# Narrow experts scatter their weighted rows into two sums by token, in place of a stage of 128 gathers

## The chip, the cores and the metric

The kernel runs on one core of a Trainium2 chip. A core has a matrix engine (TensorE, in the profile PE, with its weight loads as PEld), a vector engine (VectorE, DVE), an activation engine (ScalarE, ACT), GpSimd (POOL) and SyncE (SP), which issues most of the transfers. GpSimd issues the indirect transfers, those whose rows are picked by a list of row numbers. Sixteen DMA engines carry all transfers. The engines run side by side and wait for each other by semaphores. The metric is the device time of one execution in microseconds (us), the median of the runs.

## The reference

Four layers of cross attention and feed-forward over x, 2048 tokens of 256 numbers. The change touches the feed-forward of layer 0 (64 experts, 8 for each token, hidden width 192, at most 128 tokens an expert, beside one shared expert) and the cross attention of layer 1, which reads its result:

```
probs = softmax(x @ router_w.T);  topk_w, topk_ids = top_k(probs, 8);  topk_w /= sum(topk_w)
pos   = place of this choice among the choices of the same expert;  valid = pos < 128
idx   = topk_ids * 128 + pos                      # the slot; a token without one is dropped
x_buf[idx] = x[tok]
h = silu(x_buf @ w_gate) * (x_buf @ w_up);  y = h @ w_down           # for each expert's 128 slots
routed = segment_sum(y[idx] * topk_w * valid, tok)
x = x + routed + shared_expert(norm(x))
x = x + L1_attention(norm(x), ctx_1024)
```

## The kernel before

x stays in on-chip memory as 16 tiles of 128 tokens (`all_x`, in code `k.x`). The program is a row of stages, each a block in which every engine runs its own list and at whose end all engines meet; `begin_stage` and the SP loop of `sem_clear` free the semaphores of the last one.

**a0** (`low_rank_attention`) is the attention of layer 0, the routing of its experts and the shared expert. One loop over `step` runs all of them with a lag for each: VectorE ranks tile t in step t+6 (`rank_top` to `rank_sum`), TensorE counts it in step t+7 (`count`, which reads `chosen` and the running total `sofar`), VectorE makes its slots in step t+8 (`pick` to `place`), and GpSimd then scatters the tile's normalized rows eight times, once for each choice (`scatter`), into the slot buffer `m_xbuf` in DRAM. GpSimd also takes the power of each tile's variance (`power`, result `a_rstd`), four steps before. `rank_chosen(t)` waits for `count(t-1)`, since `chosen` and `sofar` have two buffers. Behind the loop come the shared expert (`shared_gate_up`, `hide`, `shared_down`, `add_shared`) and the weights of all tiles at once.

**m0e** (`narrow_experts`) goes over 32 pairs of experts. SP waits for all scatters, then loads a pair's rows (`load_x`, 256 KB), its gate and up weights (`load_gu`, 768 KB) and its down weights (`load_d`, 384 KB). TensorE turns the rows, makes gate and up and, two steps later, down. VectorE copies the result to `y`, and GpSimd stores it to `m_ybuf` (256 KB, one transfer a pair).

**m0c** (`combine`) gathers for every token its eight result rows: GpSimd issues 16 x 8 indirect reads of 128 rows, VectorE multiplies each by its weight and adds it to x. Beside them, in the same block, `fold_contexts` prepares the layers 1 to 3: TensorE and ACT fold the context into 33 heads' weights, SP stores them, and behind the last head SP loads three rows that VectorE splits into bf16 parts. In VectorE's list this split stands behind all adds.

**n** (`norm_scales`) takes mean and power for all tiles. **a1** (`attention`, no experts of its own) is a `pipeline` over the tiles: norm (lag 0), scores (1), masks, maxima and exp (2), output (3). A hardware loop runs its middle steps. SP has nothing to do in it but load the fold at its start and then the first weights of the next stage (`local.load_first`). The attention behind M2 (**a3**) has `combine_before` in its loop already: it gathers two rows a token and adds them in the same pipeline, all its own phases two steps later (`lag = 2`).

What orders the work is the written order of each list and the semaphores; there is no planner.

Of the kernel before, what the change touches and what calls it, by code (L numbers as in the profile page):

```python
# [360 lines left out]
def zero_slot_buffers(k, pool, names):  # L361

    for name in names:
        if name in k.slot_buffers:
            xbuf, zeroed, n, tile = k.slot_buffers[name]
            for i in range(n):
                pool.dma_start(xbuf[i * 4 * tile:(i + 1) * 4 * tile, :].rearrange("(p a) d -> p (a d)", p=tile), k.zeros[0:tile, :]).then_inc(zeroed, 16)


class Ahead:  # L370
# [3 lines left out]
    def __init__(self, k, m, d):  # L374
# [6 lines left out]
        if m is M0:  # L381
            self.slots, self.weights = s.sb("slots", [P, T, m.top], U32), s.sb("weights", [P, T, m.top])
            s = Scope(k, self.early, m.name + "w")
            self.xn_t = s.sb("xnall", [P, DC, T * P])
            self.top, self.pos = s.sb("top", [P, T, 8]), s.sb("pos", [P, T, m.top])
            self.rows = [s.sb(f"rows{i}", [P, D]) for i in range(6)]
            self.scattered = s.lasting_sems("scattered", len(self.rows))
            self.wgu = [s.sb(f"wgu{i}", [P, 2 * DC, 2 * m.hidden]) for i in range(4)]
            self.wgu_in = s.lasting_sems("wguin", len(self.wgu))
        self.wr, self.logits = s.sb("wr", [P, DC, m.e]), s.sb("logits", [P, T, m.e])  # L390
# [10 lines left out]
    def wait_scattered(self, eng):  # L401
        n = len(self.rows)
        for i in range(n):
            eng.wait_ge(self.scattered[i], 16 * self.m.top * len(range(i, T, n)))

# [43 lines left out]
def attention(nc, k, a, d):  # L449
# [6 lines left out]
    with ExitStack() as ctx:  # L456
# [61 lines left out]

        if before:
            K = before.m.top  # L520
# [5 lines left out]
            combined = s.steps("combined", *(f"{i}" for i in range(K)), "stats", "copy", "aggr", "mean", "eps")  # L526
# [7 lines left out]
        with nc.Block() as block:  # L534
            @block.sync
            def _(sp):
# [27 lines left out]
            def _(dve):  # L564
# [15 lines left out]
                def combine_before(t, u):  # L580
# [3 lines left out]
                    for i in range(K):  # L584
                        nc.vector.scalar_tensor_tensor(row(k.x, t), got[u][:, i, :], before.weights[:, bass.ts(t, 1), i], row(k.x, t),
                                                       ALU.mult, ALU.add).then_inc(combined.sem, 1)
                        done(f"{i}")
# [92 lines left out]
                masks = [(2, mask_scores if a.mask == "tokens" else mask_keys)] if a.mask else []  # L680
                if ahead:
                    for st in (renormed, logged):
                        dve.sem_inc(st.sem, 2 * st.n)
                    if before:
                        for st in (indexed, combined):
                            dve.sem_inc(st.sem, 2 * st.n)
                        for u in range(2):
# [2355 lines left out]
```

## Time and profile before

| | us |
|---|---|
| median of 3 runs | 2836.45 (2835.34 to 2838.21) |
| the profiled execution | 2839.5 |
| its span | 2837.7 |
| TensorE busy in it | 2382.7 (84%) |
| VectorE, ACT, GpSimd busy | 1223.7, 1067.9, 608.6 |
| granted TensorE clock, mean | 0.881 of 2.4 GHz |

The span runs from the first instruction to the last. The stages of the change lie in its first quarter: a0 from 0 to 303 us, m0e to 499, m0c to 690, n to 693, a1 to 762. A busy share tells how long an engine worked, not whether anything waited for it; that stands in the rows below, in the idle time before an instruction and what ended it.

### The profile page before, as it was taken

Reading aid. Unit: us, or ns where it says so; the run is one execution under the profiler, and the core shown is the slowest. Engines: PE = TensorE matmul, PEld = TensorE weight load, DVE = VectorE, ACT = ScalarE, POOL = GpSimd, SP = SyncE. Lnnn points to the kernel's source line nnn. Section 1 sums busy time; section 2 is a strip of 40 time slices with the busy share of each in tenths; the row PEclk is TensorE's granted clock in tenths of the full one; section 3 lists DMA queues with packets and bytes.
Section 4 is the critical chain, followed back from the end, with each engine's and each line's share of the span. In section 5 each row is a group of like instructions: output and inputs, shape, how many; then the busy total and the mean of one; then the engine's idle time right before and its main releaser. Section 6 shows DMA issues by size and latency. Waiting matters only on the chain. (4 is left out here: it accounts for less than half of the span.)

```text
span 2837.7 us, 44374 instructions
## 1 busy us (share of the span) xinstructions
PE 2382.7 (84%) x13334; PEld 1720.2 (61%) x13367; DVE 1223.7 (43%) x3165; ACT 1067.9 (38%) x3643; POOL 608.6 (21%) x638
## 2 busy tenths in 40 slices
PE   6996899880879989899989799549997998099991
PEld 3774577550456755467655466449985566099991
DVE  3674222344657753266743344512222564332223
ACT  2551222340256652166642255223332554033440
POOL 3277211674032110012110000130001220400004
PEclk7987999765599999999999899769998999599996
DMA  9200697542040020000000500311013300511113
GB/s 324 80 13 29 197 305 223 170 125 64 33 141 10 10 55 0 31 8 10 11 6 0 186 21 0 118 61 31 29 30 126 131 14 10 169 36 35 37 35 95
DMA packets 162724, 213.46 MB, mean 75 GB/s; under 512 B 36732, under 2 KB 140171, under 8 KB 161400
## 3 DMA queue, kind: packets, MB, share of 16 engines
q1 hardware_dynamic: 133320, 150.16, 16.8%
q0 software_dynamic: 29264, 61.54, 6.5%
q8 instruction: 74, 1.21, 0.2%
q14 instruction: 66, 0.54, 0.1%
HBM read 150.96 MB, written 83.52 MB: 83 GB/s over the span
## 5 line engine op out<-in xcount | busy, mean ns | idle before, releaser
L2321 POOL TENSOR_TENSOR la_invnorm<-la_clamped,all_minushalf 128x16 f32<-128x16 f32 x32 | 92.9, 2902 | 541.8 <-DVE la_clamped L2393 541.8
L819 PE MATMUL a_score_bank<-a_fold,a_xnt 128*128 (+3 forms) x448 | 183.7, 537 | 0.0
L846 PE MATMUL a_out_bank<-a_vw,a_probst 128*128 (+5 forms) x672 | 169.9, 406 | 3.6 <-ACT a_probst L755 3.4
L738 ACT ACTIVATE a_probs<-a_score_bank,a_mx 128x77 f32<-128x77 f32 x528 | 162.1, 363 | 3.4 <-DVE a_mx L633 2.6
L2048 ACT ACT_TABLE_LOAD x40 | 51.3, 1283 | 287.8 <-PE m3e_h_bank L2021 152.6
L2021 PE MATMUL m2e_h_bank<-m2e_xt,m2e_w1e 128*128 128x108 f32 x1280 | 152.0, 278 | 0.1
L2021 PE MATMUL m3e_h_bank<-m3e_xt,m3e_w1e 128*128 128x128 f32 x1280 | 151.7, 277 | 0.0
L2021 PEld LDWEIGHTS m2e_h_bank<-m2e_xt,m2e_w1e 128*128 128x128 f32 x1280 | 148.6, 195 | 0.5 <-DVE m2e_xt L2062 0.5
L2021 PEld LDWEIGHTS m3e_h_bank<-m3e_xt,m3e_w1e 128*128 128x128 f32 x1280 | 148.5, 194 | 0.1
L846 PEld LDWEIGHTS a_out_bank<-a_vw,a_probst 128*128 128x128 f32 (+2 forms) x672 | 129.7, 200 | 28.2 <-issue 6.8
L2031 PE MATMUL m2e_y_bank<-m_w,m2e_ht 128*108 x640 | 144.6, 379 | 0.0
L2031 PE MATMUL m3e_y_bank<-m_w,m3e_ht 128*128 x640 | 144.6, 379 | 0.0
L2471 ACT ACTIVATE la_probs<-la_score_bank,la_nb,la_invnorm 128x256 f32<-128x256 f32 x256 | 140.8, 576 | 5.8 <-DVE la_nb L2411 5.7
L2101 POOL DMA_INDIRECT m0c_got<-m_ybuf,m0c_slot x128 | 129.7, 1013 | 51.6 <-issue 44.5
L1008 POOL DMA_INDIRECT m_xbuf<-m0w_rows,m0w_slots x128 | 127.4, 995 | 37.6 <-issue 37.3
L738 ACT ACTIVATION_READ_ACCUMULATOR a_probs<-a_score_bank,a_mx 128x1 f32 x528 | 129.2, 245 | 0.0
L2031 PEld LDWEIGHTS m3e_y_bank<-m_w,m3e_ht 128*128 128x128 f32 x640 | 118.6, 190 | 14.5
L2031 PEld LDWEIGHTS m2e_y_bank<-m_w,m2e_ht 128*108 128x108 f32 x640 | 107.8, 173 | 24.1
L2048 ACT ACTIVATE m3e_ht<-m3e_h_bank,m3w_b 128x128 f32<-128x128 f32 x320 | 89.3, 376 | 85.9 <-PE m3e_h_bank L2021 85.7
L2048 ACT ACTIVATE m2e_ht<-m2e_h_bank,m2w_b 128x108 f32<-128x108 f32 x320 | 84.1, 359 | 89.5 <-PE m2e_h_bank L2021 89.2
L819 PEld LDWEIGHTS a_score_bank<-a_fold,a_xnt 128*128 128x128 f32 x448 | 82.0, 213 | 52.4 <-issue 42.1
L709 POOL DMA_INDIRECT a_got<-m_ybuf,a_slot x32 | 32.8, 1025 | 359.9 <-DVE a_slot L578 311.3
(444 smaller groups left out, 4839.1 us busy)
## 6 DMA issues: line engine op xcount, KB each, us to landing
m0w_wgu<-in_m_gu SPq DMA_DIRECT2D x32, 768.0 KB, 5.6
m_xbuf<-all_zeros POOLq DMA_DIRECT2D x36, 512.0 KB, 19.2
m_w<-in_m_w SPq DMA_DIRECT2D x16, 1024.0 KB, 12.3
m_xbuf<-all_zeros POOLq DMA_DIRECT2D x20, 432.0 KB, 11.8
m0e_wd<-in_m_down SPq DMA_DIRECT2D x32, 256.0 KB, 5.1
m0e_xb<-m_xbuf SPq DMA_DIRECT2D x32, 256.0 KB, 5.7
m_ybuf<-m0e_y POOLq DMA_DIRECT2D x32, 256.0 KB, 4.8
m2w_w<-in_m_w SPq DMA_DIRECT2D x8, 1024.0 KB
```

The lines of the kernel that those rows point to most:

```text
L709: nc.gpsimd.indirect_dma_start(got[u][:, i, :], None, before.ybuf[:, :], bass.IndirectOffsetOnAxis(slot[u][:, i:i + 1], 0), bounds_check=b ...
L738: last = nc.scalar.activation(probs[u][:, h * J:(h + 1) * J], score_ps[g][:, (h - h0) * J:(h - h0 + 1) * J], ACT.Exp, bias=mx[u][:, h:h + ...
L819: last = nc.tensor.matmul(score_ps[g][:, (hs[0] - h0) * J:(hs[-1] + 1 - h0) * J].rearrange("p (h j) -> p h j", j=J), xn_t[u][:, c, :], fol ...
L846: last = nc.tensor.matmul(out_ps[:, 0:D], probs_t[u][0:n, c, :], vw[0:n, bass.ds(b, 1), c, :].rearrange("p o n -> p (o n)"), start=False, ...
L1008: nc.gpsimd.indirect_dma_start(k.slot_buffers[m.name][0][:, :], bass.IndirectOffsetOnAxis(ahead.slots[:, t, i:i + 1], 0), ahead.rows[t % R ...
L2021: last = nc.tensor.matmul(h_ps[u][half][:, i * R:(i + 1) * R], w1[u][:, c, f0:f0 + P], xt[u][:, c, :], start=c == 0, stop=c == DC - 1)
L2031: last = nc.tensor.matmul(y_ps[u][0:R, 0:D], h_t[u][:, c, :], r.w2[:, bass.ts(e, 1), c, :].rearrange("p o f -> p (o f)"), start=c == 0, st ...
L2048: last = nc.scalar.activation(h_t[u][:, 4 * half + i, :], h_ps[u][half][:, i * R:(i + 1) * R], m.act, bias=r.ahead.b1[:, bass.ds(e * HC + ...
L2101: nc.gpsimd.indirect_dma_start(got[u][:, j, i, :], None, r.ybuf[:, :], bass.IndirectOffsetOnAxis(slot[u][:, j, i:i + 1], 0), bounds_check= ...
L2321: nc.gpsimd.tensor_tensor(inv_norm[t % 2][:, :], clamped[t % 2][:, :], k.minus_half[:, :], ALU.pow).then_inc(powered.sem, 1)
L2471: last = nc.scalar.activation(probs[u][:, hh, :], score_ps[j][:, i * 2 * P:(i + 1) * 2 * P], ACT.Exp, bias=nb[u][:, hh:hh + 1], scale=inv_ ...
```

## The change

The expert stage no longer stores its results by slot. Each row of `m_xbuf` grows from 256 to 288 numbers (`PAYLOAD`): behind the token's row it carries the eight expert numbers, the eight weights and the token's number. In m0e VectorE finds in a loaded row the weight that belongs to this expert and the token (`find`, `found_at`; an empty slot gets one of 128 spare rows), multiplies the result by the weight (`copy_y`), and GpSimd scatters it with an adding transfer into one of two DRAM tensors of 2560 rows by token, `sums[0]` for the first expert of a pair and `sums[1]` for the second. Two adds into one tensor must not overlap, so each waits for the one before. The sums start as x (stored by SP at the end of a0) and zero. m0c is left with the folds alone (`fold_stage`), n goes, and a1 loads both sums tile by tile and adds them (`combine_before` with `summing`).

In a0 the weights are made tile by tile (`rank_shift`, `soften`, `carry`), `sofar` has three buffers and `rank_chosen(t)` waits for `count(t-2)`, and the first two of four parts of the shared expert's gate and up move into the last steps of the loop.

```diff
@@ a0, SP, behind the first weights
                 for q in range(len(ahead.wgu)):
                     ahead.load_gate_up(sp, q)
+                ahead.wait_scattered(sp)
+                for q in range(len(ahead.xb)):
+                    ahead.load_rows(sp, q)
+                sp.wait_ge(ahead.sum_zeroed, 96)
+                for p in range(T // 2):
+                    sp.wait_ge(shared_added, p + 1)
+                    sp.dma_start(ahead.sums[0][1 + 2 * p * P:1 + 2 * (p + 1) * P, :].rearrange("(t p) d -> p t d", p=P),
+                                 k.x[:, 2 * p:2 * p + 2, :]).then_inc(ahead.x_stored, 16)
@@ a0, GpSimd, behind the zeroing of the slots
+                for i, total in enumerate(ahead.sums):
+                    for c in range(0 if i else SUM_ROWS // 512 - 1, SUM_ROWS // 512):
+                        pool.dma_start(total[c * 512:(c + 1) * 512, :].rearrange("(p a) d -> p (a d)", p=P), k.zeros[:, 0:4 * D]).then_inc(ahead.sum_zeroed, 16)
...
                 def scatter(t):
                     pool.wait_ge(placed, t + 1)
+                    pool.wait_ge(weighing, 2 * (t + 1))
@@ a0, VectorE
+                def carry(t):
+                    dve.wait_ge(softened, t + 1)
+                    nc.vector.reciprocal(sum_top[t % 2][:, :], sum_top[t % 2][:, :]).then_inc(weighing, 1)
+                    nc.vector.tensor_scalar(ahead.rows[t % R][:, IDS], idxf[t % 3][:, :], 1.0, None, ALU.add)
+                    nc.vector.tensor_copy(ahead.rows[t % R][:, TOKEN], k.token[:, t:t + 1])
+                    dve.wait_ge(weighing, 2 * t + 1)
+                    nc.vector.tensor_scalar(ahead.rows[t % R][:, WEIGHTS], exped_top[t % 2][:, :], sum_top[t % 2][:, 0:1], None, ALU.mult).then_inc(weighing, 1)
...
                 def rank_chosen(t):
                     dve.wait_ge(ranked, 5 * t + 4)
-                    if t >= 1:
-                        dve.wait_ge(counted, t)
-                        dve.wait_ge(summed, t)
+                    if t >= 2:
+                        dve.wait_ge(counted, t - 1)
@@ a0, TensorE, in the loop over the steps
+                    if step == T + 3:
+                        pe.wait_ge(shared_in, 48)
+                        pe.wait_ge(exped, NG * T)
+                        pe.wait_ge(p_copied, 3 * T)
+                        shared_gate_up(0)
+                    if step == T + 6:
+                        pe.wait_ge(added, T)
+                        pe.wait_ge(logged, T)
+                        shared_gate_up(1)
@@ m0e, SP
                 def load_x(q):
-                    if q >= NX:
-                        sp.wait_ge(turned, q - NX + 1)
-                    sp.dma_start(xb[q % NX][:, :, :], r.xbuf[q * 2 * P:(q + 1) * 2 * P, :].rearrange("(i p) d -> p i d", p=P)).then_inc(x_in[q % NX], 16)
+                    sp.wait_ge(turned, q - NX + 1)
+                    sp.wait_ge(found, 2 * (q - NX + 1))
+                    r.ahead.load_rows(sp, q)
@@ m0e, GpSimd
                 for q in range(npair):
                     pool.wait_ge(y_copied, q + 1)
-                    pool.dma_start(r.ybuf[q * 2 * P:(q + 1) * 2 * P, :].rearrange("(i p) d -> p i d", p=P), y[q % 2][:, :, :]).then_inc(stored[q % 2], 16)
-                for u in range(2):
-                    pool.wait_ge(stored[u], 16 * (npair // 2))
+                    for i in range(2):
+                        if q >= 1:
+                            pool.wait_ge(summed[i], 16 * q)
+                        nc.gpsimd.indirect_dma_start(sums[i][:, :], bass.IndirectOffsetOnAxis(dest[q % NY][:, i:i + 1], 0), y[q % NY][:, i, :], None,
+                                                     bounds_check=SUM_ROWS - 1, oob_is_err=True, compute_op=ALU.add).then_inc(summed[i], 16)
@@ m0e, VectorE
                 def copy_y(q):
                     dve.wait_ge(y_made, q + 1)
-                    if q >= 2:
-                        dve.wait_ge(stored[q % 2], 16 * (q // 2))
-                    nc.vector.tensor_copy(y[q % 2][:, :, :].rearrange("p i d -> p (i d)"), y_ps[q % 2][:, :]).then_inc(y_copied, 1)
+                    dve.wait_ge(found, 2 * (q + 1))
+                    for i in range(2):
+                        last = nc.vector.tensor_scalar(y[q % NY][:, i, :], y_ps[q % 2][:, i * D:(i + 1) * D], weight[q % NY][:, i:i + 1], None, ALU.mult)
+                    last.then_inc(y_copied, 1)
@@ a1, SP
+                if summing:
+                    for i in range(2):
+                        sp.wait_ge(before.ahead.summed[i], 16 * (M0.ntiles // 2))
+                    def load_sums(t, u):
+                        sp.wait_ge(combined.sem, combined.at(t - 2, "x"))
+                        for i in range(2):
+                            sp.dma_start(got[u][:, i, :], before.ahead.sums[i][bass.ds(t * P + 1, P), :]).then_inc(gathered[u], 16)
+                    pipeline(sp, T, (0, load_sums))
                 if local:
                     local.load_first(sp)
@@ a1, VectorE
-                    pipeline(dve, T, *later((0, norm), *masks, (2, maxima), (2, scale), (3, add)))
+                    pipeline(dve, T, *later((0, norm), *masks, (2, maxima)), *combine_first, *later((2, scale), (3, add)))
```

Three places show how instructions move. First SP's list at the end of a0 and the start of m0e, before (L408 is `load_gate_up`, L1836 `load_x`):

```order
L408 DMA m0w_wgu<-in_m_gu 128x4x384 x4
L961 UNCONDITIONAL_BRANCH
L1828 UNCONDITIONAL_BRANCH
...
L1847 DMA m0e_wdrest<-in_m_down 64x2x256
L1836 DMA m0e_xb<-m_xbuf 128x2x256 x5
```

and in the change (L1038 stores x into the first sum):

```order
L419 DMA m0w_wgu<-in_m_gu 128x4x384 x4
L415 DMA m0w_xb<-m_xbuf 128x2x288 x4
L1038 DMA m_sum<-all_x 128x2x256 x8
L1004 UNCONDITIONAL_BRANCH
L1912 UNCONDITIONAL_BRANCH
...
L1931 DMA m0e_wdrest<-in_m_down 64x2x256
L415 DMA m0w_xb<-m_xbuf 128x2x288
L419 DMA m0w_wgu<-in_m_gu 128x4x384
```

The first four loads of rows move ahead of the seam between the stages (the two branches) and of the down weights, and eight stores stand between them and the seam.

GpSimd's list from m0e to the end of m0c, before:

```order
L1862 DMA m_ybuf<-m0e_y 128x2x256 x32
L1827 UNCONDITIONAL_BRANCH
L2092 UNCONDITIONAL_BRANCH
...
L2101 DMA m0c_got<-m_ybuf,m0c_slot 128x256
L2098 REGISTER_ALU
```

and in the change:

```order
L1948 DMA m_sum<-m0e_y,m0e_dest 2560x256 x64
L1911 UNCONDITIONAL_BRANCH
L724 UNCONDITIONAL_BRANCH
L730 TENSOR_TENSOR all_rstd<-all_var,all_minushalf 128x1
L83 UNCONDITIONAL_BRANCH
```

32 stores become 64 adds, the 128 gathers are gone, and L730 takes the power of a tile's variance in a1.

VectorE's list for one step of a1 (the last one ahead of the hardware loop, from the masks on), before:

```order
L622 TENSOR_TENSOR a_score_bank<-a_score_bank,a_factor 128x77
L624 TENSOR_TENSOR a_score_bank<-a_score_bank,a_addend 128x77
L633 TENSOR_REDUCE a_mx<-a_score_bank 128x1
L639 RECIPROCAL a_inv<-a_total 128x1
L641 TENSOR_TENSOR a_probs<-a_probs,a_inv 128x77
L645 TENSOR_TENSOR all_x<-all_x,a_out_bank 128x256
L647 BN_STATS all_stats<-all_x 128x6
```

and in the change:

```order
L659 TENSOR_REDUCE a_mx<-a_score_bank 128x1
L606 TENSOR_TENSOR all_x<-a_got 128x256
L614 BN_STATS all_stats<-all_x 128x6
L617 COPY a_stb<-all_stats 128x6
L620 BN_AGGR a_mvb<-a_stb 128x2
L623 COPY all_mean<-a_mvb 128x1
L624 TENSOR_SCALAR all_var<-a_mvb 128x1
L665 RECIPROCAL a_inv<-a_total 128x1
L667 TENSOR_TENSOR a_probs<-a_probs,a_inv 128x77
L671 TENSOR_TENSOR all_x<-all_x,a_out_bank 128x256
```

Six instructions, each waiting for the one before, move in between the maximum and the reciprocal of every step.

## Rows read from the trace of the kernel before

**Rows 1.** Stretches of a0's loop, of m0c's fold and of a1.

```profile
core 0: us, PE busy (x) PEld busy (x) DVE busy (x) ACT busy (x) POOL busy (x), PEclk, DMA share, GB/s
124.00:203.00 79.00, 78.89 (x428) 56.17 (x426) 60.62 (x191) 42.04 (x165) 62.01 (x64) 0.87 0.09 27
507.00:632.00 125.00, 122.90 (x548) 78.03 (x548) 49.27 (x110) 55.37 (x185) 95.95 (x95) 0.69 0.50 151
699.00:762.00 63.00, 55.38 (x176) 33.47 (x176) 36.46 (x128) 17.20 (x65) 0.00 (x0) 0.50 0.28 91
```

**Rows 2.** GpSimd in order of time, a0: start, duration, then idle time and its releaser.

```profile
124.41 1.10 POOL L1008 DMA_INDIRECT m_xbuf<-m0w_rows,m0w_slots  x1 [0.19 <-issue]
...
191.54 0.89 POOL L1003 TENSOR_TENSOR a_rstd<-a_ve,all_minushalf 128x1 f32<-128x1 f32 x1 [0.17 <-DVE a_ve L1109]
...
296.80 0.97 POOL L1008 DMA_INDIRECT m_xbuf<-m0w_rows,m0w_slots  x1 [0.30 <-issue]
```

**Rows 3.** VectorE in order of time, one step of a0's loop.

```profile
189.60 1.04 DVE L1144 TENSOR_REDUCE a_chosen<-a_onehot 128x64 bf16<-128x512 f32 x1 [2.82 <-issue]
...
191.31 0.14 DVE L1109 TENSOR_SCALAR a_ve<-a_mv 128x1 f32<-128x1 f32 x1
```

**Rows 4.** SP's issues in order of time, first of m0e.

```profile
303.47 0.37 SPq L1846 DMA_DIRECT2D m0e_wd<-in_m_down  x1
...
308.69 6.66 SPq L1836 DMA_DIRECT2D m0e_xb<-m_xbuf  x5
```

**Rows 5.** TensorE in order of time, first of m0e.

```profile
313.85 1.97 PE L1876 MATMUL m0e_turned_bank<-all_ident,m0e_xb 128*128 128x128 f32 x8 [13.56 <-DMA m0e_xb<-m_xbuf]
```

**Rows 6.** One y store of m0e, in GpSimd's order of time.

```profile
459.80 0.72 POOL L1862 DMA_DIRECT2D m_ybuf<-m0e_y  x1 [4.87 <-DVE m0e_y L1948]
```

**Rows 7.** A stretch inside m0e, columns as in rows 1.

```profile
330.00:386.00 56.00, 56.00 (x362) 42.57 (x360) 14.34 (x30) 13.51 (x30) 7.18 (x10) 1.00 1.02 308
```

**Rows 8.** DMA between 325 and 500 us, rate in 40 equal slices.

```profile
GB/s 347 345 311 289 305 329 315 306 287 309 315 325 285 288 326 302 317 291 300 320 320 307 278 320 319 287 304 288 336 315 288 303 306 314 28 37 60 60 60 60
```

**Rows 9.** From issue to landing: the 32 stores of m0e's y.

```profile
DMA to landing us min/median/max: 2.5/4.8/6.0
```

**Rows 10.** From issue to landing: the 128 scatters of a0.

```profile
DMA to landing us min/median/max: 2.1/2.2/3.6
```

**Rows 11.** GpSimd in order of time, the last gather of m0c.

```profile
676.41 1.00 POOL L2101 DMA_INDIRECT m0c_got<-m_ybuf,m0c_slot  x1 [0.30 <-issue]
```

**Rows 12.** TensorE in order of time, first of the fold.

```profile
506.93 1.39 PE L290 MATMUL m0c_kv_bank<-all_ctxt,m0c_a1wk 128*128 128x154 f32 x4 [12.54 <-DMA m0c_a1wo<-in_a_wo]
```

**Rows 13.** ACT in order of time, last of the fold.

```profile
632.24 0.57 ACT L340 COPY m0c_vwout<-m0c_v_bank 77x512 f32<-77x512 f32 x1
```

**Rows 14.** VectorE in order of time, end of m0c, stage n, a1's first norm.

```profile
683.41 0.15 DVE L349 CAST m0c_a1part<-m0c_a1row 82x5 bf16<-82x5 f32 x1
...
686.08 0.18 DVE L357 CAST m0c_a3part<-m0c_a3rest 85x32 bf16<-85x32 f32 x1
690.85 1.17 DVE L158 BATCH_NORM_AGGREGATE all_mv<-all_stats 128x2 f32<-128x6 f32 x16 [4.59 <-PEq L2091]
...
698.92 0.73 DVE L605 TENSOR_SCALAR a_xn<-all_x,all_mean,all_rstd 128x256 f32<-128x256 f32 x2
```

**Rows 15.** VectorE in order of time, one step of a1's loop.

```profile
719.53 0.42 DVE L645 TENSOR_TENSOR all_x<-all_x,a_out_bank 128x256 f32 x1 [0.32 <-PE a_out_bank L846]
...
721.47 0.24 DVE L633 TENSOR_REDUCE a_mx<-a_score_bank 128x1 f32<-128x77 f32 x1
722.19 0.16 DVE L639 RECIPROCAL a_inv<-a_total 128x1 f32<-128x1 f32 x1 [0.48 <-ACT a_probs L738]
...
723.16 0.42 DVE L645 TENSOR_TENSOR all_x<-all_x,a_out_bank 128x256 f32 x1 [0.54 <-PE a_out_bank L846]
```

**Rows 16.** VectorE in order of time, the same chain in a3's loop.

```profile
2314.01 0.48 DVE L585 SCALAR_TENSOR_TENSOR all_x<-a_got,all_m2weights,all_x 128x256 f32 x1 [0.16 <-DVE all_x L585]
...
2316.08 0.15 DVE L598 TENSOR_SCALAR all_var<-a_mvb 128x1 f32 x1
2316.30 0.17 DVE L654 COPY a_st<-all_stats 128x6 f32 x1
```

More of the change, by code:

```diff
@@ L517, in attention @@
             routed, logged = s.steps("routed"), s.steps("logged")
+        summing = before is not None and before.m is M0
         if before:
-            K = before.m.top
+            K = 2
             got, slot = s.pair("got", [P, K, D]), s.pair("slot", [P, K], U32)
@@ L525, in attention @@
             indexed, scaled_before = s.steps("indexed"), s.steps("scaledbefore")
-            combined = s.steps("combined", *(f"{i}" for i in range(K)), "stats", "copy", "aggr", "mean", "eps")
+            combined = s.steps("combined", *(("x",) if summing else ("0", "x")), "stats", "copy", "aggr", "mean", "eps")
         def later(*phases):
@@ L583, in combine_before @@
                     dve.wait_ge(gathered[u], (t - u) * (8 * K) + 16 * K)
[L584 to L587, printed above, removed]
+                    if summing:
+                        nc.vector.tensor_tensor(row(k.x, t), got[u][:, 0, :], got[u][:, 1, :], ALU.add).then_inc(combined.sem, 1)
+                    else:
+                        for i in range(K):
+                            if i:
+                                done("0")
+                            nc.vector.scalar_tensor_tensor(row(k.x, t), got[u][:, i, :], before.weights[:, bass.ts(t, 1), i], row(k.x, t),
+                                                           ALU.mult, ALU.add).then_inc(combined.sem, 1)
+                    done("x")
                     nc.vector.bn_stats(row(k.stats, t), row(k.x, t)).then_inc(combined.sem, 1)
@@ L680, in _ @@
                 masks = [(2, mask_scores if a.mask == "tokens" else mask_keys)] if a.mask else []
+                index_first, combine_first = ([(0, index)], [(1, combine_before)]) if before else ([], [])
+                if before:
+                    for st in (indexed, combined):
+                        dve.sem_inc(st.sem, 2 * st.n)
+                    if summing:
+                        index_first = []
+                    else:
+                        for u in range(2):
+                            nc.vector.memset(got[u][:, :, :], 0.0).then_inc(cleared, 1)
                 if ahead:
@@ L1021, in _ @@
                 nc.vector.memset(none3[:, :], 0.0)
+                for rows in ahead.rows:
+                    nc.vector.memset(rows[:, D:PAYLOAD], 0.0)
                 nc.vector.tensor_copy(before16[:, :], k.before[:, :])
@@ L1955, in narrow_experts, with fold_stage @@
         r.old_sems.close()
+def fold_stage(nc, k, jobs):
+    with ExitStack() as ctx:
+        with nc.Block() as block:
+            fold_contexts(nc, k, Scope(k, ctx, "m0c"), block, jobs)
 def wide_experts(nc, k, m, d, r):
@@ L2156, in experts @@
         r.xbuf, r.zeroed, r.nzero, _ = k.slot_buffers[m.name]
-        r.ybuf = nc.dram_tensor(f"{m.name}_ybuf", (m.rows, D), F32, kind="Internal").ap()
+        if m is not M0:
+            r.ybuf = nc.dram_tensor(f"{m.name}_ybuf", (m.rows, D), F32, kind="Internal").ap()
         r.iota, r.before, r.ones = k.iota, k.before, k.ones
         r.m = m
-        if m is M0:
-            r.slots, r.weights = k.ahead.slots, k.ahead.weights
-        elif m is M2:
+        if m is M2:
             r.slots, r.weights = k.m2_slots, k.m2_weights
-        else:
+        elif m is M3:
             r.slots, r.weights = s.sb("slots", [P, T, m.top], U32), s.sb("weights", [P, T, m.top])
```

233 lines of the change are left out of this document (143 added, 90 removed).

## The prediction

> **What bounds the kernel now.** I read the stretches by window first, since each stage of the change has a limit of its own. In a0's loop TensorE is busy for 78.89 of 79 us, GpSimd for 62.01 [rows 1]: it is TensorE's loop. In m0e TensorE is again never idle (56.00 of 56), but the DMA engines are busy all the time too, share 1.02 at 308 GB/s [rows 7], so two limits lie side by side. In the fold TensorE works 122.9 of 125 us at a clock of 0.69, in a1 55.38 of 63 at 0.50, which is the lower level, 1.2 GHz [rows 1].
>
> Then the rows at the seams, for who comes last. From the last scatter to TensorE's first turn in m0e 17 us pass, of which TensorE waits 13.56 for the rows [rows 2, 5]. The fold's last copy ends at 632.8 [rows 13], but the split behind it stands in VectorE's list behind all adds, whose last gather is issued at 676.41 [rows 11]; it runs at 683.41 [rows 14]. So m0c ends with the chain of gathers and adds, 50 us after the fold. That tail is where time can be had.
>
> **Part 1, a0's loop.** GpSimd's scatters wait for slots, these for `chosen`, and that for the last count: 2.82 us of wait in one step [rows 3]. The power at 191.54 is the last thing in GpSimd's list that waits for VectorE; from there the scatters run back to back to 296.80 [rows 2]. So only what makes the list late before 191.54 counts. The wait of 2.82 goes; `carry` puts four small instructions ahead of the slots and takes back some 0.3. Term: -2.5 us (ends -3 and 0). Rows of 288 numbers in place of 256 are 12.5% more bytes; an issue of 0.97 to 1.10 us [rows 2] is work on 128 row numbers, not on bytes, so I cost it at 0; were it by bytes, 128 x 0.12 = +15 us, which I keep for the range. The early zeroing (about 4 MB more in a0) has nobody waiting and 0.09 of the DMA engines in use [rows 1]: 0. The two parts of the shared expert that move into the loop take its end ahead of the last scatter; a loop that TensorE bounds grows by them, but GpSimd, not TensorE, ends the stage: 0.
>
> **Part 2, the seam.** From 296.80 to 313.85 it is 17.05 us [rows 2, 5]. Now SP waits for the scatters (landing 2.2 [rows 10]) and issues four loads and eight stores before it meets the others; eight issues took 5.22 us (303.47 to 308.69 [rows 4]), so 12 x 0.65 = 7.8, and some 0.7 for the seam itself. The rows have landed by then. 2.2 + 7.8 + 0.7 = 10.7: term -6.3 (ends -9 and -3). What is late next is SP itself with its stores.
>
> **Part 3, m0e.** A pair takes 0.72 + 4.87 = 5.59 us [rows 6] and moves 768 + 256 + 128 KB of weights, 256 of rows in and 256 of y out, 1664 KB, 305 GB/s, which fits the 308 of the row. Now the rows are 288 KB, and an add reads its destination too: 1696 + 256 = 1952 KB. The trace has no adding transfer, so bounds. The best rate in m0e is 347 GB/s [rows 8]; 1952 KB at 346 is 5.78 us, +0.19 for each of 32 pairs, +6. If TensorE's 5.59 hides everything, 0. If an add costs its bytes once more (2208 KB), 6.53 us, +30. Slices of 345 are the first two only, when buffers are empty; the others lie at 285 to 335, so I take 5.95, that is 336 GB/s: +12 (ends 0 and +30).
>
> A rule of the Trainium skill bears on this ("Collectives: The Full Stack", The bandwidth ceiling): a reducing transfer is slower than a copy not for the addition but because it reads two sources, one descriptor for each. By that rule it is 1952 KB and +6; no row here shows an add, and my +12 does not rest on it.
>
> Beside the rate there is a chain. Each add waits for the last one into its tensor, so each of the two tensors must take its 128 KB within a period. A y store of 256 KB lands in 4.8 us under this load and at most in 6.0 [rows 9], a scatter of 128 rows under light load in 2.2 [rows 10]. With a landing under 5.5 the chain is hidden; I take it as hidden, at about 5 us, near the store's 4.8. GpSimd's issues, 2 x 1.0 us, fit. VectorE's extra (`find`, `found_at`) too: it worked 14.34 of 56 us [rows 7].
>
> The Trainium skill ("DMA: Bandwidth & Descriptors", Anatomy of one DMA) gives 2.0 us and the bytes at 436 GB/s for one: 2.3 us for 128 KB and 2.6 for twice that. The scatter's 2.2 agrees, the store's 4.8 does not, since it has no load of others in it; the chain would by it be hidden with room to spare.
>
> **Part 4, the seam to the fold.** The fold's first matmul stands 12.54 us idle, on a weight load [rows 12], behind a stage end at which GpSimd waited for y stores. That wait goes to a1: -1.5 (ends -4, 0).
>
> **Part 5, m0c.** TensorE's fold is as long as before and its clock, with TensorE busy 98%, the same. From its last copy at 632.8: store and reload of rows, two issues and landings of 2.2 to 2.5 each, 5.5 in all; the splits 683.41 to 686.26, 2.85; to the next block 4.59 [rows 14]. 632.8 + 5.5 + 2.85 + 4.6 = 645.75, where it was 690.85: -45 (ends -40, -52). What is late next is the fold itself. The last adds have landed 130 us earlier.
>
> **Part 6, n and a1.** Stage n goes, 8.07 us from 690.85 to a1's first norm at 698.92 [rows 14]. In its place a1 waits for the loads of the sums (an issue, a landing of 2.2), sum, statistics and power before its first norm, about 8 as well: 0. In its loop a step takes 3.63 us, add to add [rows 15]: 2.18 from the add to the end of the maximum, 0.48 of wait for ACT's exp, 0.97 to the next add, of which 0.54 is waiting for TensorE. The sum, the copies and statistics come behind the maximum, each waiting for the one before; in a3 the same chain takes 2.3 us (2314.01 to 2316.30) [rows 16]. It covers both waits: 2.18 + 2.3 + 0.49 = 4.97 with the 0.54 gone and 0.48 covered, about 1.3 a step more. Term: 15 x 1.3 = +19.5 (ends: it hides further in waits, +8; it hides in nothing, 15 x 2.3 = +34). The first weights of the next stage are issued behind 14 tiles' loads, some 20 us later in a stage that then lasts over 80: hidden (0, +3).
>
> **Sum.** -2.5 - 6.3 + 12 - 1.5 - 45 + 19.5 = -23.8 us against the profiled execution's 2839.5. The median of the runs is 2836.45, 0.1% under it, so I take the difference from that: 2812.6.
>
> **Rival 1, the adds cost nothing.** TensorE never waits in m0e, and a share of 1.02 with rates up to 347 [rows 7, 8] does not prove a full limit. Then m0e stays at 5.59 a pair and the term of +12 goes: 2836.45 - 35.8 = 2801. Against it: the rate falls whenever buffers are full, and 17% more bytes come.
>
> **Rival 2, slower: the chain of adds is the bound.** Each add reads, adds and writes 128 rows of 1 KB in the full queues of m0e; if its landing is over the period, period = landing + 0.3, and the pairs stretch, TensorE waits for `y` buffers or rows. Without Part 3 the rest gives -35.8, so it turns to slower from a period of 5.59 + 35.8/32 = 6.71, a landing of 6.4. For it: the store reached 6.0 with one trip to memory [rows 9], an add needs two. At a landing of 7.3, +64.6 - 35.8 = +29: 2865. Against it: it is half the bytes of the store.
>
> **Rival 3, the steps of a1 hide nothing** and the first weights come late: +34 + 3 in place of 19.5, 2830; with scatters 12% dearer it would be 2845. For it: a chain of six dependent instructions on an engine that is already the slow one with TensorE at 0.50. Against it: the waits are in the rows.
>
> **Chances.** Forecast (2805 to 2825) 0.46, rival 1 (2795 to 2805) 0.18, rival 3 (2826 to 2840) 0.12, rival 2 (2837 and up) 0.17, anything else 0.07, spread on both sides. 0.2%, 5.7 us, is what can be told from no change here. Faster by more: forecast, rival 1 and nearly all of the 2830s short of 2830.8 (0.08), with some of the rest, 0.77; within 0.2% 0.05; slower 0.18. The range 2792 to 2846 leaves out some 0.13 above and 0.04 below; the forecast's own is 2805 to 2825.
>
> **What would show it.** First scatter and power of tile 6 about 2.5 us earlier; TensorE's first turn of m0e near 305, with SP issuing stores right up to it; period of pairs 5.8 to 6.1, with TensorE's idle time put down to weights or rows (rate limit), not to `y` (chain): GpSimd waiting for its own add before nearly every issue, at a period equal to the landing, would prove rival 2. The fold's end then 45 us nearer to a1; a1's step at 4.9 with no idle before the reciprocal; the first weights of the stage behind a1 landed before it begins. It is wrong if m0e's period stays 5.6 or passes 6.5, or a1's step passes 5.5.

## The result, and the profile after

| | before | changed |
|---|---|---|
| median, 8 runs each | 2836.69 us | 2849.79 us |
| range | 2833.29 to 2843.23 | 2842.42 to 2859.85 |
| time to before | | 1.0045 (95%: 1.0028 to 1.0062) |
| span of the profiled execution | 2837.7 | 2848.2 |

Slower by 0.45%, where 2812.6 was forecast: the range that was given held neither the time nor, with its 0.77 for faster, the direction. The mechanism that decides is the second rival, the chain of adds. These are the points in time in both profiled executions, from rows like those below ([rows 2, 5, 12 to 14] for before); the differences add up to the spans' 10.5 us.

| | before | changed | difference | forecast |
|---|---|---|---|---|
| start to first scatter | 124.4 | 118.9 | -5.5 | none |
| first to last scatter | 172.4 | 170.4 | -2.0 | -2.5 |
| to the first matmul of m0e | 17.05 | 11.17 | -5.9 | -6.3 |
| m0e's matmuls | 180.5 | 218.5 | +38.0 | +12 |
| their end to the fold | 12.5 | 27.6 | +15.1 | -1.5 |
| fold to a1's first norm | 192.0 | 148.0 | -44.0 | -45 |
| a1, first norm to last addition | 62.5 | 76.9 | +14.4 | +19.5 |
| the rest | 2076.3 | 2076.7 | +0.4 | 0 |

The changed kernel's GpSimd list in the middle of m0e, in order of time (start, duration, then the idle time before it and what ended it):

```profile
376.99 1.54 POOL L1948 DMA_INDIRECT m_sum<-m0e_y,m0e_dest  x1 [5.68 <-DMA m_sum<-m0e_y,m0e_dest]
378.83 1.54 POOL L1948 DMA_INDIRECT m_sum<-m0e_y,m0e_dest  x1 [0.30 <-issue]
384.75 1.54 POOL L1948 DMA_INDIRECT m_sum<-m0e_y,m0e_dest  x1 [4.38 <-DMA m_sum<-m0e_y,m0e_dest]
386.60 1.54 POOL L1948 DMA_INDIRECT m_sum<-m0e_y,m0e_dest  x1 [0.30 <-issue]
392.36 1.54 POOL L1948 DMA_INDIRECT m_sum<-m0e_y,m0e_dest  x1 [4.22 <-DMA m_sum<-m0e_y,m0e_dest]
```

In [rows 6] the idle time ahead of the store was ended by VectorE's result. Here it is ended by GpSimd's own last add. A pair takes 392.36 - 384.75 = 7.61 us where it took 5.59; from 376.99 to 506.98 us seventeen pairs take 7.65 each. The two adds of the list go into different tensors. These are the views of the one at 384.75, into the tensor of the pair's second expert, and of the one at 386.60, into the first's:

```profile
L1948 POOL DMA_INDIRECT m_sum<-m0e_y,m0e_dest x1: 1541/1541/1541, 384.8 to 384.8; - x1
...
DMA to landing us min/median/max: 6.8/6.8/6.8
```

```profile
L1948 POOL DMA_INDIRECT m_sum<-m0e_y,m0e_dest x1: 1541/1541/1541, 386.6 to 386.6; - x1
...
DMA to landing us min/median/max: 5.8/5.8/5.8
```

The first of them lands at 391.6 (landings are counted from the start of the issue), and the next add into its tensor is issued 0.8 us later, at 392.36: 6.8 + 0.8 is the period. The other tensor has 1.8 us to spare. So one of the two chains sets the pace. The view of that line over all of m0e says how long an add takes and who waited for it:

```profile
L1948 POOL DMA_INDIRECT m_sum<-m0e_y,m0e_dest x64: 1532/1540/1575, 313.0 to 534.2; - x64
...
  DMA m_sum<-m0e_y,m0e_dest: 110.9, 32
...
  DVE m0e_weight L2047: 120.6, 23
  POOL m_sum L1948: 110.9, 32
DMA to landing us min/median/max: 3.6/6.2/8.8
```

The landing, 6.2 us in the median (6.5 between 320 and 500 us), stands where [rows 9] have 4.8 for a store of twice the bytes. GpSimd waited 110.9 us for it, and VectorE 120.6: `found_at` waits for the adds of four pairs ago before it writes `weight` and `dest`. That wait stands ahead of `hide` in VectorE's list, so `hide`, with which TensorE goes on, comes late although its data are there:

```profile
391.71 0.17 DVE L2047 TENSOR_REDUCE m0e_weight<-m0e_picked 128x2 f32<-128x16 f32 x1 [5.70 <-DMA m_sum<-m0e_y,m0e_dest]
391.80 0.15 DVE L2048 TENSOR_TENSOR m0e_dest<-m0e_spot,m0w_xb 128x2 uint32<-128x2 f32 x1
391.86 0.41 DVE L2026 TENSOR_TENSOR m0e_hrest<-m0e_gaterest,m0e_gu_bank 64x256 f32<-64x256 f32 x1
```

By windows, the columns as in [rows 1], the stretch of [rows 7] and the next one, changed kernel:

```profile
330.00:386.00 56.00, 54.56 (x335) 41.84 (x334) 17.49 (x79) 12.13 (x27) 22.80 (x15) 0.94 0.90 252
386.00:440.00 54.00, 47.35 (x263) 35.42 (x262) 13.33 (x64) 10.20 (x23) 22.41 (x16) 0.91 0.85 232
```

The DMA share falls from 1.02 to 0.85 and the rate from 308 to 232 GB/s. So it is not the engines' rate that ran out; they wait too. Behind the last matmul GpSimd still has a backlog: matmul, last add, and TensorE's first matmul of the fold:

```profile
518.22 0.70 PE L1986 MATMUL m0e_y_bank<-m0e_wdrest,m0e_hrest 64*128 64x256 f32 x2
```

```profile
534.19 1.54 POOL L1948 DMA_INDIRECT m_sum<-m0e_y,m0e_dest  x1 [0.30 <-issue]
```

```profile
546.57 1.39 PE L290 MATMUL m0c_kv_bank<-all_ctxt,m0c_a1wk 128*128 128x154 f32 x4 [27.65 <-DMA m0c_a1wo<-in_a_wo]
```

The last add is issued 15.3 us behind the last matmul (518.92), and no engine leaves the stage before it: the fold's first load is issued at 540.76. That is the +15.1.

The other side, ACT's last copy of the fold and VectorE's split:

```profile
670.75 0.58 ACT L340 COPY m0c_vwout<-m0c_v_bank 77x512 f32<-77x512 f32 x1
```

```profile
676.48 0.17 DVE L349 CAST m0c_a1part<-m0c_a1row 82x5 bf16<-82x5 f32 x1 [155.38 <-DMA m0c_a3row<-a_dram_row]
...
694.55 0.41 DVE L631 TENSOR_SCALAR a_xn<-all_x,all_mean,all_rstd 128x256 f32<-128x256 f32 x1 [0.75 <-POOL all_rstd L730]
```

The split follows the fold by 5.1 us, where 50.6 lay between [rows 13, 14]; 5.5 was forecast. The stage did lose its tail.

a1, VectorE in order of time, from one addition to the next:

```profile
712.78 0.41 DVE L671 TENSOR_TENSOR all_x<-all_x,a_out_bank 128x256 f32 x1
...
714.69 0.24 DVE L659 TENSOR_REDUCE a_mx<-a_score_bank 128x1 f32<-128x77 f32 x1
714.91 0.43 DVE L606 TENSOR_TENSOR all_x<-a_got 128x256 f32 x1
...
716.89 0.15 DVE L624 TENSOR_SCALAR all_var<-a_mvb 128x1 f32 x1
716.96 0.15 DVE L665 RECIPROCAL a_inv<-a_total 128x1 f32<-128x1 f32 x1
717.15 0.24 DVE L667 TENSOR_TENSOR a_probs<-a_probs,a_inv 128x77 f32<-128x77 f32 x1
717.30 0.41 DVE L671 TENSOR_TENSOR all_x<-all_x,a_out_bank 128x256 f32 x1
```

The waits for ACT and TensorE in [rows 15] are gone; the chain of the sum takes 2.1 us (714.91 to 717.04). From 712.78 to 755.54 nine steps take 4.75 us each, where 3.63 to 3.78 stood.

### The profile page after: what moved, and what is told of

The parts are those of the page before. It is cut to its first block and busy times, and to the rows that moved or that the text cites. A ratio compares the mean times of both kernels' runs of the same rounds, so it can differ in the third digit from the quotient of the medians.

```text
span 2848.2 us, 44375 instructions
## 1 busy us (share of the span) xinstructions
PE 2407.0 (85%) x13366; PEld 1735.3 (61%) x13367; DVE 1192.0 (42%) x3352; ACT 1065.6 (37%) x3670; POOL 565.2 (20%) x564
## 3 DMA queue, kind: packets, MB, share of 16 engines
q1 hardware_dynamic: 140392, 157.51, 16.9%
## 5 line engine op out<-in xcount | busy, mean ns | idle before, releaser
L777 ACT ACTIVATE a_probs<-a_score_bank,a_mx 128x77 f32<-128x77 f32 x528 | 161.7, 360 | 16.9 <-DVE a_mx L659 16.8
L1948 POOL DMA_INDIRECT m_sum<-m0e_y,m0e_dest x64 | 98.6, 1541 | 146.9 <-DMA m_sum<-m0e_y,m0e_dest 110.9
L2528 DVE TENSOR_REDUCE la_mx<-la_score_bank 128x2 f32<-128x512 f32 x128 | 87.7, 685 | 48.2 <-PE la_score_bank L2670 48.2
```

What stands on the lines that cost most here:

```text
L777: last = nc.scalar.activation(probs[u][:, h * J:(h + 1) * J], score_ps[g][:, (h - h0) * J:(h - h0 + 1) * J], ACT.Exp, bias=mx[u][:, h:h + ...
L1948: nc.gpsimd.indirect_dma_start(sums[i][:, :], bass.IndirectOffsetOnAxis(dest[q % NY][:, i:i + 1], 0), y[q % NY][:, i, :], None, bounds_che ...
L2528: nc.vector.tensor_reduce(mx[u][:, h0:h1 + 1:2], score_ps[j][:, :].rearrange("p (h e) -> p h e", h=2), AX, ALU.max).then_inc(maxed.sem, 1)
```

## The experiments

All against the kernel before in the same set. What follows of the stages is read from one trace for each. m0e's matmuls hardly vary from one to the next (180.5 to 181.9 us wherever the stall is gone); the first scatter does (117.7 to 129.0 us).

**e1, e2: more tensors for the sums.**

The waits of `found_at` and the loads and additions of a1 follow the number of tensors.

```diff
-                        if q >= 1:
-                            pool.wait_ge(summed[i], 16 * q)
-                        ...(sums[i][:, :], ..., compute_op=ALU.add).then_inc(summed[i], 16)
+                        e = 2 * q + i
+                        o = e % NSUM                      # 3 in e1, 4 in e2
+                        if e >= NSUM:
+                            pool.wait_ge(summed[o], 16 * (e // NSUM))
+                        ...(sums[o][:, :], ..., compute_op=ALU.add).then_inc(summed[o], 16)
```

> Expert e adds into tensor e mod 3 of three, in place of two; an add waits for the one three experts earlier; the attention behind loads and adds three sums. Theory A (the chain: a tensor's next add waits for the last one's landing, 6.95 us from issue and 0.6 to the next issue, 7.55 us a pair) : the limit falls to 7.55 x 2/3 = 5.0 us a pair, so the pairs go by the matmuls or the DMA engines, 5.6 to 6.1 us; from the first to the last matmul of m0e 218 us becomes 182 to 197, and the backlog of adds behind the last matmul (17 us) is nearly gone; a1 gains one more addition a step, +0.5 x 16 = 8 us. Total 2849 - 30 - 13 + 8 = about 2810 to 2820. Theory B (the DMA engines cannot move the bytes of the adds faster): m0e stays at 218 us and the total rises by 8.

> Four tensors, an add waits for the one four experts earlier. Theory A: the chain allows 3.8 us a pair, nothing is left of it; m0e is as with three tensors or 1 to 3 us shorter, a1 8 us longer than with three, total 2815 to 2828. Theory B: m0e 218 us as with two.

e1: 2812.21 us, time to before 0.991 (0.9891 to 0.9929). e2: 2821.05 us, 0.9933 (0.9913 to 0.9953). m0e's matmuls take 180.5 and 181.7 us, what they took before the change. The waits of line L1958 (the add) in e1 and its landing:

```profile
  DVE m0e_y L2064: 62.0, 25
  DMA m_sum<-m0e_y,m0e_dest: 24.6, 17
  issue: 12.3, 22
...
DMA to landing us min/median/max: 3.7/6.8/8.6
```

and the window of m0e again, e1, beside which the kernel before had 1.00 and 307 in the last two columns:

```profile
386.00:440.00 54.00, 54.00 (x347) 41.02 (x347) 19.88 (x90) 13.23 (x30) 29.31 (x20) 1.00 1.10 316
```

The landing is as long as before, 6.8 us, and TensorE never waits, since GpSimd now waits for VectorE's result, and 24.6 us for adds instead of 110.9. Theory B, that the engines can't move the bytes of the adds faster, falls: 316 GB/s at a share of 1.10 go through, with the same adds. a1 got 7.0 us longer with the third sum (83.9) and another 7.3 with the fourth (91.2), so three is the better number.

**e3: the same transfers without the add.**

```diff
-  bounds_check=SUM_ROWS - 1, oob_is_err=True, compute_op=ALU.add).then_inc(summed[i], 16)
+  bounds_check=SUM_ROWS - 1, oob_is_err=True).then_inc(summed[i], 16)
```

> The scatters of m0e write their rows and do not add (the sum over the experts is left out); all waits are as in the changed kernel. If the add itself makes the transfer long (its destination is read), the landing falls from 6.95 us to about 5, the period to the matmuls' 5.6, and GpSimd's issue from 1.54 to about 1.0 us; total about 2805. If it is the queueing beside 1.7 MB of other transfers a pair, landing and period fall by less than a quarter: 6.5 us a pair or more, total above 2825.

It leaves out the sum over the experts. 2807.48 us, 0.9898 (0.9876 to 0.9919); m0e's matmuls 180.5 us. The line's view:

```profile
L1948 POOL DMA_INDIRECT m_sum<-m0e_y,m0e_dest x64: 979/983/992, 314.3 to 489.1; - x64
...
  DMA m_sum<-m0e_y,m0e_dest: 101.0, 37
...
  DVE m0e_weight L2047: 23.4, 12
...
DMA to landing us min/median/max: 2.4/4.7/7.5
```

The add makes the landing 1.5 us longer (6.2 against 4.7) and an issue 0.56 us longer (1.54 against 0.98). Against e1, where the pairs follow each other as fast as here, it is 2.1 us (6.8). The plain one, with the same waits, fits into the period of the matmuls; the adding one doesn't. GpSimd waits nearly as long for its own transfers as in the changed kernel (101.0 us against 110.9) and m0e loses nothing by it: what costs is the wait that reaches VectorE, 23.4 us here and 120.6 there.

The add also takes the DMA engines longer, for the same bytes. Between 330 and 470 us, e1 with 51 adds and e3 with 46 plain transfers (packets, MB, share of the 16 engines' time):

```profile
q0 software_dynamic: 7312, 6.66, 31.1%
```

```profile
q0 software_dynamic: 2255, 6.16, 11.5%
```

That is 2.4 times the engine time for one transfer. An add's 128 KB are counted once here, so the rates in GB/s hold nothing of the destination that it reads.

**e4: the same adds beside fewer bytes.**

```diff
-                    r.ahead.load_gate_up(sp, q)
+                    sp.dma_start(wgu[q % NG][:, 0:1, :], ... rows q*2*D : q*2*D + P ...)      # 192 of 768 KB
```

> The gate and up weights of each pair behind the fourth are loaded to a quarter only (192 of 768 KB; the rest is what an earlier pair left, so the results of those experts are other ones). The chain of adds and all waits stay. If the landing is long because the add shares the DMA engines with the weights, it falls towards the 4.1 us of the adds at the end of m0e, where nothing else is moved, and the pairs go at the matmuls' 5.6 us: m0e's matmuls 180 to 185 us, total 2805 to 2812. If it is long by itself, the period stays near 7.5.

It leaves out three quarters of the gate and up weights of most pairs. 2804.8 us, 0.9875 (0.9855 to 0.9896); m0e's matmuls 181.9 us. Adds land in

```profile
DMA to landing us min/median/max: 3.7/4.4/6.1
```

So the 6.2 us are both: the shortest add takes 3.6, and most of the other 2.6 is what shares the engines with it, since three quarters of the gate and up weights less take 1.8 away. The chain was 2.06 us over the matmuls' period (7.65 against 5.59), and either cause taken away ends the stall; in e4 the view shows no wait of VectorE for an add.

**e5 to e12: two chips on which a0's scatters and m0c's gathers are disturbed.** e5 to e8 and e9 to e12 came to chips on which the kernel before takes 2958.5 and 2963.4 us. e5, e6, e7 and e9 are one run each.

> In a0 rank_chosen(t) waits for count(t-1) again, as in the kernel before; all else is the changed kernel. If the earlier start of a tile's ranking is what shortens the chain of scatters, the time from the first scatter to the last is 172.4 us again, as before, and not 170.1 to 171.0 as in the five profiles with the changed a0. If GpSimd has no wait left in it anyway, it stays at 170 to 171. m0e's pairs stay at 7.5 us.

> The first two parts of the shared expert's gate and up go behind a0's loop again. If GpSimd's scatters end the stage in both cases, m0e starts as before, 11.0 to 11.2 us behind the last scatter. If the move took TensorE's shared expert off the end of the stage, the last stores of x into the first sum wait for it, and m0e starts 3 to 10 us later measured from the last scatter; the last scatter itself stays about 170 us behind the first.

Their edits are those of e14 and e15 below, made to the changed kernel. 2933.52 and 2923.11 us. The scatters take 213.5 and 218.8 us, and 37 and 36 more pass before m0e begins. Neither tells anything of its edit; e14 and e15 make the same edits to the kernel with three sums, on a chip like the first.

> All 64 adds go into one tensor, each waiting for the one before. Theory A (a chain of landings): a pair takes two landings and two turnrounds of 0.6 us. With TensorE and the weights slowed to this, the adds have less beside them, so a landing lies between the 4.1 us of the end of m0e and 6.9 us: 9.4 to 15 us a pair, m0e's 64 adds take 300 to 480 us, total 2930 to 3100. If the adds were held by the rate of the engines and not by waits, the period stays at 7.5 and m0e as in the changed kernel.

e7 (the edit of e1 with NSUM = 1): 3061.94 us. m0e depends little on the disturbance (its matmuls take 221.3 to 229.3 us with two sums on these chips, where the first had 218.5, and 180.5 to 181.9 with three), and this is the clearest look at the chain. GpSimd, in order of time:

```profile
506.51 1.54 POOL L1958 DMA_INDIRECT m_sum<-m0e_y,m0e_dest  x1 [5.59 <-DMA m_sum<-m0e_y,m0e_dest]
511.06 1.54 POOL L1958 DMA_INDIRECT m_sum<-m0e_y,m0e_dest  x1 [3.01 <-DMA m_sum<-m0e_y,m0e_dest]
518.09 1.54 POOL L1958 DMA_INDIRECT m_sum<-m0e_y,m0e_dest  x1 [5.48 <-DMA m_sum<-m0e_y,m0e_dest]
522.61 1.54 POOL L1958 DMA_INDIRECT m_sum<-m0e_y,m0e_dest  x1 [2.98 <-DMA m_sum<-m0e_y,m0e_dest]
```

A pair is a short and a long add, 4.55 + 7.03 = 11.6 us. The one at 506.51 has nothing beside it, the one at 511.06 the loads that SP issues from 510.66 on:

```profile
DMA to landing us min/median/max: 3.7/3.7/3.7
```

```profile
DMA to landing us min/median/max: 6.2/6.2/6.2
```

Each costs its landing and 0.8 us (4.55 - 3.7 and 7.03 - 6.2); that is the turnround, where the second rival had 0.3.

> Three sums, and in a1 the statistics of the combined rows are kept in small tensors of their own, so that two of the seven dependent instructions of a step go (the copy of the statistics and the copy of the mean). If a1's step is VectorE's list, it falls by 0.35 to 0.6 us from e1's, 84 us to 75 to 79 from the first normalized tile to the last addition; total 2803 to 2807 where three sums alone had 2812. If the step is set by another wait, it stays at 2812.

e8 edits a1, on top of e1 (norm and power then read the small tensors):

```diff
-                    nc.vector.bn_stats(row(k.stats, t), row(k.x, t)).then_inc(combined.sem, 1)
-                    done("stats")
-                    nc.vector.tensor_copy(st6_before[u][:, :], row(k.stats, t)).then_inc(combined.sem, 1)
-                    done("copy")
+                    nc.vector.bn_stats(st6_before[u][:, :], row(k.x, t)).then_inc(combined.sem, 1)
+                    done("stats")
                     nc.vector.bn_aggr(mv_before[u][:, :], st6_before[u][:, :]).then_inc(combined.sem, 1)
                     done("aggr")
-                    nc.vector.tensor_copy(col(k.mean, t), mv_before[u][:, 0:1]).then_inc(combined.sem, 1)
-                    nc.vector.tensor_scalar(col(k.var, t), mv_before[u][:, 1:2], LN_EPS, None, ALU.add)
+                    nc.vector.tensor_scalar(var_before[u][:, :], mv_before[u][:, 1:2], LN_EPS, None, ALU.add)
```

2872.81 us, 0.9706 (0.9678 to 0.9734). a1 takes 76.3 us, 7.6 less than in e1; what it brings on the first chip is in e16.

> The kernel before, for a second profile: where its a0, m0e, m0c and a1 stand on the chip of this set. Where the chip is as in e1 to e4: first to last scatter 172 us, m0e's matmuls 180.5, fold's last copy to split 50 us. Where it is as in e5 to e8 (a0's scatters 207 to 219 us, 36 to 41 us from the last one to m0e): both of these long here too, so that they have nothing to do with the change, and the 128 gathers of m0c longer than their 180 us.

> The changed kernel, for its stages on the chip of this set and for the comparison with the two below. Period of m0e's pairs 7.5 us, m0e's matmuls 218 to 229 us. Time to before 1.0045 where transfers by row number go as in e1 to e4; about 0.99 where they are slow as in e5 to e8, since then 128 gathers fall away that cost more there.

> Three sums as in e1: m0e's matmuls 180 to 182 us, 30 to 38 us less in total than e10.

> Three sums and the shorter chain as in e8. a1 from its first normalized tile to its last addition was 76.3 us in e8 against 83.9 in e1: 7 us less in total than e11, so 2805 where e1 has 2812.

e9, the kernel before: 2967.14 us. Its scatters take 202.5 us and the seam 50, so the long a0 is not the change's doing. And its fold, which runs beside the gathers, takes 234 us in place of 126, with all engines idle more often (compare [rows 1], 507 to 632 us, where TensorE is busy 98%). e9 by windows:

```profile
570.00:640.00 70.00, 26.11 (x103) 14.59 (x102) 23.92 (x54) 7.22 (x23) 50.98 (x50) 0.55 0.34 100
640.00:720.00 80.00, 48.78 (x156) 26.57 (x156) 29.07 (x67) 13.62 (x46) 54.39 (x55) 0.54 0.19 53
```

e10, the changed kernel: 2930.1 us, 0.9901 (0.987 to 0.9931), its fold 122 us, since no gathers run beside it, and m0e nearly as slow as on the first chip (matmuls 221.3 us). So on such a chip the change is 1% faster, and on the first 0.45% slower, with the same loss in m0e. e11: 2877.38 us, 0.9713 (0.9656 to 0.977), 53 us under e10, where 30 to 38 were expected; m0e's matmuls and the wait behind them give 49 of it in the traces, and a1 takes 7 back, so the rest is not explained. e12: 2875.79 us, 0.9699 (0.9662 to 0.9736); the 7 us expected between these two can't be told there. Why engines stop beside these transfers the traces do not show: 78.6 us of ACT's idle time in e9's fold end at what the profile calls "remote", which names no instruction. That they go by row number is not enough, since the 64 adds of m0e do too and run as on the first chip. Nor do the runs tell whether it is the chip itself or what else ran on it then. It stays open.

**e13 to e16: the parts of a0, and the shorter chain, on a chip like the first** (before 2837.35 us).

> The base of this set: three sums as in e1, against which the three below are read. On a chip like that of e1: 2812; on one like that of e11: 2877.

> Three sums, and rank_chosen(t) waits for count(t-1) again. If this wait was worth what the prediction says, first to last scatter is 172.4 us, 2 us more than in the base, and the total 2 to 3 us more. If the a0 of the changed kernel is as fast without it, no difference.

> Three sums, and the first two parts of the shared expert's gate and up behind a0's loop again. TensorE's shared expert ended 4 us behind the last scatter in the changed kernel; with 13.6 us of matmuls behind the loop again, whose waits of TensorE in the last steps come back instead, it ends some 5 to 14 us later, so m0e starts up to 10 us later measured from the last scatter, and the total is 3 to 10 us above the base. If GpSimd's scatters end the stage anyway, there is no difference; that is what the prediction said (0).

> Three sums and the shorter chain in a1. In the traces a1 is 7.6 us shorter than with three sums alone; if nothing takes that back, the total is 5 to 9 us below the base.

All four have the three sums of e1; e15 moves `hide` of these parts behind the loop as well.

```diff
 e14, rank_chosen
-                    if t >= 2:
-                        dve.wait_ge(counted, t - 1)
+                    if t >= 1:
+                        dve.wait_ge(counted, t)
 e15, TensorE
-                    if step == T + 3: ... shared_gate_up(0)
-                    if step == T + 6: ... shared_gate_up(1)
+                shared_gate_up(0)                          # behind the loop
+                shared_gate_up(1)
```

| | median | time to before | first scatter | first to last | to m0e | a1 |
|---|---|---|---|---|---|---|
| e13 three sums | 2810.75 | 0.9907 (0.9883 to 0.9931) | 120.1 | 170.5 | 11.45 | 83.9 |
| e14 and old wait | 2821.04 | 0.9934 (0.9913 to 0.9955) | 129.0 | 173.0 | 11.11 | 83.9 |
| e15 and gate behind loop | 2812.59 | 0.9914 (0.9892 to 0.9936) | 122.4 | 171.0 | 10.85 | 83.9 |
| e16 and short chain | 2802.4 | 0.988 (0.9857 to 0.9902) | 117.7 | 171.3 | 10.78 | 76.4 |

The old wait comes back as such: in e14 `chosen` waits for the count 16.9 us between 120 and 300 us, and the chain of scatters is 2.5 us longer, as forecast. But the total is 10 us more, where 2 to 3 were expected, and each of e14's five runs is above all four of e13. In the trace the first scatter is 8.9 us later, with a lower granted clock between 60 and 125 us, e14 and e13:

```profile
60.00:125.00 65.00, 65.00 (x318) 43.98 (x317) 35.02 (x98) 34.69 (x139) 2.85 (x4) 0.80 0.58 218
```

```profile
60.00:125.00 65.00, 65.00 (x372) 46.60 (x372) 44.40 (x129) 38.89 (x160) 8.02 (x9) 0.93 0.59 223
```

Whether that comes of the wait can't be said: e2 and e12, without it, had clocks of the same kind there and first scatters at 128.1 and 128.0. The move of the gate and up is worth nothing that can be told here (e15), as forecast: TensorE's last matmul of a0 ends 3.1 us later than in e13 (301.1 against 298.0), but the last scatter is 2.8 later too (293.4 against 290.6), and m0e starts 10.85 us behind it, as in the others. The 5 to 14 us that were expected for TensorE did not come.

e16 is the version that beats both kernels: 2802.4 us, 1.2% under the kernel before.

## Why the prediction was wrong, by its own steps

**Part 3, the chain.** The step that failed is the sentence "I take it as hidden, at about 5 us, near the store's 4.8". It measured 6.5 in m0e's full stretch (median of both tensors), and 6.8 to 6.9 in the tensor that sets the pace. The nearest row was taken for the value, a store that only writes, although the bounds on the table (2.2 light, 6.0 under load at most, for one trip to memory) held the limit of 5.5 above which the chain shows. e3 shows the missing part, +1.5 us for the add; e4 the load's part. The second error is the turnround: 0.3 us was allowed from a landing to the next issue, and 0.8 (e7) is what it takes. The landing in the slower tensor and 0.8 come to the 7.65 measured; by the second rival's landing + 0.3, with the 6.5, it would be 6.8. The issue, 1.54 us where 1.0 was entered, adds nothing, since it lies inside the landing.

The chance of 0.17 was low for a step whose limit of 5.5 lay inside its own bounds, with the 6.4 that turns the sign just above their 6.0. The rival's +65 for a period of 7.6 us was too high all the same: the first pairs ran ahead into the four `y` buffers, and the last adds, with no loads beside them, took 4.5 us a pair (511.50, 516.03 and 520.53 us). It is 53 us, 38 in the matmuls and 15 behind them, of which 5.9 stay in e1 without the chain.

**Part 3, the rate.** The +12 was not there either. With the chain out of the way (e1, e2) m0e's matmuls take 180.5 to 181.7 us, 0 to 1.1 more than before, at 315 to 316 GB/s and a share of 1.10 in e1. A share of about 1.0 in [rows 7] was read as a limit and was none: the first rival was right in this term. The sum also put a pair's 1952 KB, the read destinations among them, against rates in GB/s that, as e1 shows, leave these reads out. The rule of the Trainium skill ("Collectives: The Full Stack", The bandwidth ceiling) that an add is slower for its second source agrees in kind with e3, where the landing is 1.5 us shorter without the add and a transfer takes the engines less than half the time; the +6 that it would have made of the rate did not show. The other one ("DMA: Bandwidth & Descriptors", Anatomy of one DMA), 2.3 us for 128 KB, agrees with e3's shortest landing of 2.4 and not with its median of 4.7: its two terms hold nothing for the load of others.

**Part 4** had the wrong sign even without the chain: 18.4 us from the last matmul to the fold in e1 against 12.5 [rows 12]. The prediction counted the wait for stores that goes, and forgot that the last adds are issued one by one behind the last matmul (the last at 484.89 in e1, 5.5 us behind it), and that all engines wait there for GpSimd.

**Parts 1, 2, 5 and 6 held**: -2.0 for -2.5 (e14: 2.5 for the wait), -5.9 for -6.3, -44.0 for -45, +14.4 for +19.5. In a1 the sum takes 2.1 us in place of 2.3, and the step 4.75 in place of 4.97. The -5.5 ahead of the first scatter is no part of the change as far as can be told: the first scatter stands at 117.7 to 129.0 us in the profiles of the chips like the first.

That three sums come to the forecast's number (2812.2 and 2810.8 for 2812.6) is chance: 12 too much in m0e, 7 too little behind it (+5.9 in e1 for -1.5), and 2 too little in a1, where the third sum's 7 us met the 5 by which the step had been costed too high; the rest is in the parts that no change explains, such as the first scatter.

## What to carry to other kernels

When a plain transfer becomes an adding one that must wait for the last one into the same place, the budget is no longer bytes per period but latency per tensor: landing under the load of that stage, counted from the issue, plus turnround. Work out first from which landing on the chain shows, and if that lies between the shortest and the longest landing in the trace, spend one more destination; here a third one cost 7 us and gave back 47 (246.1 us from m0e's first matmul to the fold, 198.9 in e1). Look then at what stands behind the wait in its engine's list, since VectorE's wait for old adds held back `hide`, and at whether the queue is empty when the stage ends.

## What the runs showed of the hardware

- An adding transfer by row number (128 rows of 1 KB) costs GpSimd 1.54 us to issue, a plain one 0.98, and lands in 3.6 us at the least, a plain one in 2.4; beside 1.5 MB of other transfers a pair, in 6.2 to 6.8 and 4.7 (medians of m0e). It takes the DMA engines 2.4 times as long (e1, e3). From a landing to the next issue 0.8 us pass.
- A DMA share of 1.0 is not the end: 1.10 at 316 GB/s was measured with no more waiting.
- The same program takes 2837 us on one chip and 2958 to 2963 on two others, whatever the cause. There the scatters of a0 took 30 to 53 us longer, the seam behind them 17 to 33, and the fold beside the gathers 108 (e9); the other stages of e9 and e10 are as on the first to within 3 us. The same change is 0.45% slower on one chip and 1% faster on another, since what it takes away costs differently there.
